# A fused attention and feed-forward layer on eight cores: feed-forward weight loads prefetched one block ahead through smaller staging buffers, and the closing layernorm taken two token tiles at a time

## The reference, cut to what matters

```python
# per sequence: x is 2048 tokens x 2048 features, float32
x = layernorm(x + attention(x))                  # 16 heads, latent q and kv, causal softmax
g   = (x @ gate_w.T) * gate_s                    # 5632 hidden features
u   = (x @ up_w.T) * up_s
hdn = silu(g) * u
x = layernorm(x + (hdn @ down_w.T) * down_s)     # eps 1e-5, no weights
```

## Time and profile before

| what | us |
|---|---|
| median of the 2 timed runs | 5615.35 (5584.98 and 5645.73) |
| the profiled execution | 5474.59 |
| its span on the slowest core (core 3) | 5472.8 |
| spans of the 8 cores | 5415.7 to 5472.8 |
| TensorE busy, share of the span | 3874.9, 71% |
| VectorE busy | 1907.8, 35% |
| ScalarE busy | 1626.9, 30% |

### The profile page before, as it was taken

One profiled execution on the slowest core, in us unless ns is written; L12 is line 12 of the kernel. 1 busy time (PEld: TensorE's weight loads), 2 busy tenths in 40 slices (PEclk: granted clock), 3 DMA queues, 4 the chain that ended last, 5 costly groups with the idle time before them and its releaser, 6 DMA issues.

```text
span 5472.8 us, 67555 instructions; the slowest of 8 cores (5415.7 to 5472.8 us)
## 1 busy us (share of the span) xinstructions
PE 3874.9 (71%) x20400; PEld 1835.9 (34%) x20400; DVE 1907.8 (35%) x4134; ACT 1626.9 (30%) x3184; POOL 318.4 (6%) x581
## 2 busy tenths in 40 slices
PE   0566577666666666666477698868879688868986
PEld 0223232233333333333133233333334233433343
DVE  2222223544444444443233333233322333233323
ACT  0011100035555555555101233223322233223322
POOL 0000000000000000000000011111111111101111
PEclk9877788878888788877688899989999899989998
DMA  4111111000000000000411588758876788758975
GB/s 124 54 39 32 55 53 47 14 14 7 7 7 9 7 7 7 8 2 25 138 39 47 177 269 252 251 177 261 254 246 215 210 254 249 244 181 253 272 236 180
DMA packets 207283, 673.46 MB, mean 123 GB/s; under 512 B 30240, under 2 KB 30752, under 8 KB 202848
## 3 DMA queue, kind: packets, MB, share of 16 engines
q1 hardware_dynamic: 120528, 340.64, 20.6%
q0 software_dynamic: 78928, 310.68, 18.0%
q10 hardware_dynamic: 7488, 17.83, 1.2%
HBM read 652.01 MB, written 16.78 MB: 122 GB/s over the span
## 4 chain that ended last, share of the span: by engine, by line
PE 36%; DMA 33%; DVE 12%; issue 10%; ACT 7%; DVEq 1%; SPq 0%; ACTq 0%; POOL 0%; POOLq 0%
DMA stg_gp<-up_l 21%; PE pD L1178 6%; PE pPT L584 5%; DMA stg_gp<-down_c 5%; PE pOP L964 5%; PE pQA L494 3%; ACT Ebuf L869 3%; PE pO L818 3%; ACT PTsb L841 3%; PE pPT L834 2%; DVE ubf L244 2%; PE pS L781 2%; PE pS L792 2%; DMA stage<-ow_l 2%; DVE stats L799 2%
## 5 line engine op out<-in xcount | busy, mean ns | idle before, releaser
L1095 PE MATMUL pG<-OX,gbf 128*128 128x512 bf16 x2816 | 676.9, 396 | 292.4 <-DVE tmid L1122 277.7
L1178 PE MATMUL pD<-h_fm,dbf 128*128 128x512 bf16 x2816 | 642.4, 385 | 114.4 <-DVE dbf L244 75.9
L1104 PE MATMUL pU<-OX,ubf 128*128 128x512 bf16 x2816 | 636.5, 379 | 0.0
L244 DVE CAST ubf<-stg_gp 128x1024 bf16<-128x1024 f32 x352 | 243.6, 693 | 963.1 <-DMA stg_gp<-up_l 922.3
L235 ACT CAST gbf<-stg_sy 128x1024 bf16<-128x1024 f32 x352 | 353.9, 1043 | 647.7 <-PE pG L1095 572.9
L1095 PEld LDWEIGHTS pG<-OX,gbf 128*128 128x128 bf16 x2816 | 276.8, 101 | 681.3 <-issue 402.1
L818 PE MATMUL pO<-PTsb,vtm 128*128 128x128 bf16 x2176 | 240.4, 240 | 313.4 <-ACT PTsb L841 307.1
L1178 PEld LDWEIGHTS pD<-h_fm,dbf 128*128 128x128 bf16 x2816 | 274.5, 99 | 460.8 <-issue 165.4
L841 ACT CAST PTsb<-pPT 128x512 bf16<-128x512 f32 (+3 forms) x640 | 313.0, 525 | 270.9 <-PE pPT L834 270.3
L1104 PEld LDWEIGHTS pU<-OX,ubf 128*128 128x128 bf16 x2816 | 275.6, 98 | 332.2
L869 ACT ACTIVATE Ebuf<-pS,stats 128x512 bf16<-128x512 f32 (+3 forms) x512 | 314.3, 621 | 207.0 <-DVE stats L860 201.9
(11 more groups left out here) (133 smaller groups left out, 3744.4 us busy)
## 6 DMA issues: line engine op xcount, KB each, us to landing
stg_gp<-up_l POOLq DMA_DIRECT2D x352, 512.0 KB, 6.4
stg_sy<-gate_l SPq DMA_DIRECT2D x352, 512.0 KB, 6.6
stg_sy<-down_c SPq DMA_DIRECT2D x128, 512.0 KB, 6.1
stg_gp<-down_c POOLq DMA_DIRECT2D x128, 512.0 KB, 5.5
stg_sy<-down_c SPq DMA_DIRECT2D x64, 384.0 KB, 7.1
stg_gp<-down_c POOLq DMA_DIRECT2D x64, 384.0 KB, 4.1
stage<-x SPq DMA_DIRECT2D x64, 256.0 KB, 3.1
xst<-x POOLq DMA_DIRECT2D x16, 1024.0 KB, 5.1
```

Source lines behind the costliest of these rows:

```text
L244: e.tensor_copy(d[:, a:a + cc], tiles[i][:, 0:cc]), inc=cP)
L1095: P.op("tensor", lambda e, wi=wi, d=d, gc0=gc0: e.matmul(pG[wi][:], gbf[wi][:, d * 128:(d + 1) * 128], OX[:, d * S + gc0:d * S + gc0 + 512 ...
L1104: P.op("tensor", lambda e, wi=wi, d=d, gc0=gc0: e.matmul(pU[wi][:], ubf[wi][:, d * 128:(d + 1) * 128], OX[:, d * S + gc0:d * S + gc0 + 512 ...
L1178: P.op("tensor", lambda e, di=di, hh=hh, jj=jj, ii=ii: e.matmul(pD[di][:], dbf[hh][:, jj * 128:(jj + 1) * 128], h_fm[:, ii * 512:(ii + 1) ...
```

## The change

Four things are done in the feed-forward half; the arithmetic is the same.

- `gu_loads` runs one block ahead: block 0 at the head of each group, block `ii + 1` behind the matmuls of `ii`. Nothing of the next group is loaded ahead of the down stage.
- The staging slots shrink: `gp` from 2x1024 to 2x768 columns, `sy2` from 3x1024 to 3x512. A block of up is then 3 chunks (768, 768, 512) where it was 2, of gate 4 where it was 2; a half of down is 4 chunks on `gp` (3 before) and 6 on `sy2` (3 before).
- `outst` is two buffers, with a semaphore each for their stores.
- The layernorm takes the 4 token tiles as two pairs, each step for both tiles of a pair before the next step.

```diff
-            outst = [sbF("outst0", [128, D], F32)] * 2
+            outst = [sbF("outst0", [128, D], F32), sbF("outst1", [128, D], F32)]
...
-            lc_gp = mk_path(sbF, "gp", "gpsimd", "vector")
-            lc_sy = mk_path(sbF, "sy2", "sync", "scalar", nslots=3)
+            lc_gp = mk_path(sbF, "gp", "gpsimd", "vector", slot_cols=768)
+            lc_sy = mk_path(sbF, "sy2", "sync", "scalar", nslots=3, slot_cols=512)
...
-            pre2 = {0: gu_loads(0), 1: gu_loads(1)}
             for grp in range(NGRP):
                 gc0 = grp * 512
...
+                pre = gu_loads(0)
...
-                    g_ready, u_ready = pre2.pop(ii)
+                    g_ready, u_ready = pre
...
-                    if ii + 2 < IC:
-                        pre2[ii + 2] = gu_loads(ii + 2)
+                    if ii + 1 < IC:
+                        pre = gu_loads(ii + 1)
...
-                if grp + 1 < NGRP:
-                    pre2[0] = gu_loads(0)
-                    pre2[1] = gu_loads(1)
...
-                for tc in range(4):
+                for pair0 in (0, 2):
+                    tcs = (pair0, pair0 + 1)
...
-                    out_free[0] = out_free[1] = (dOut, dOut.n)
+                    for tc in tcs:
+                        t_abs = grp * 4 + tc
+                        sem_o = dOut if tc % 2 == 0 else dOut2
+                        P.w("gpsimd", vE, ap[tc])
+                        P.op("gpsimd", lambda e, t_abs=t_abs, tc=tc: e.dma_start(
+                            out=out_hbm[t_abs * 128:(t_abs + 1) * 128, :],
+                            in_=outst[tc % 2][:]), inc=sem_o, k=16)
+                        out_free[tc % 2] = (sem_o, sem_o.n)
```

More of the change, by code:

```diff
@@ L148, in build_program @@
         dOut = P.sem("dOut")
+        dOut2 = P.sem("dOut2")
         dDump = P.sem("dDump")
@@ L1074, in build_program, with gu_loads @@
             HALF = IC // 2
[L1076 to L1082, removed]
-            pre2 = {0: gu_loads(0), 1: gu_loads(1)}
             for grp in range(NGRP):
                 gc0 = grp * 512
+                def gu_loads(ii):
+                    wi = ii % 2
+                    P.wf("scalar", gbf_free[wi])
+                    g_ready = lc_sy(gate_l[ii], gbf[wi], 0, D)
+                    P.wf("vector", ubf_free[wi])
+                    u_ready = lc_gp(up_l[ii], ubf[wi], 0, D)
+                    return g_ready, u_ready
+                pre = gu_loads(0)
                 P.w("tensor", vE, a4_done_v)
@@ L1201, in build_program @@
                 h_free = (tMM, d_mm)
-                for tc in range(4):
-                    t_abs = grp * 4 + tc
+                for pair0 in (0, 2):
+                    tcs = (pair0, pair0 + 1)
+                    bs = {tc: 10 + 6 * (tc % 2) for tc in tcs}
                     P.w("vector", vE, x2tm_ready)
-                    P.op("vector", lambda e, tc=tc: e.reduce_sum(
-                        stats[:, 10:11], x2tm[:, tc * D:(tc + 1) * D], axis=AX), inc=vStat)
-                    P.w("vector", vStat, vStat.n)
[L1208 to L1211, removed]
+                    for tc in tcs:
+                        b = bs[tc]
+                        P.op("vector", lambda e, tc=tc, b=b: e.reduce_sum(
+                            stats[:, b:b + 1], x2tm[:, tc * D:(tc + 1) * D],
+                            axis=AX), inc=vStat)
+                    P.w("vector", vStat, vStat.n)
+                    for tc in tcs:
+                        b = bs[tc]
+                        P.op("vector", lambda e, b=b: e.tensor_scalar_mul(
+                            stats[:, b + 1:b + 2], stats[:, b:b + 1], -1.0 / D), inc=vStat)
+                        P.op("vector", lambda e, b=b: e.tensor_scalar_mul(
+                            stats[:, b + 4:b + 5], stats[:, b:b + 1], 1.0 / D), inc=vStat)
                     nm_done = vStat.n
@@ L1214, in build_program @@
                     P.w("scalar", vStat, nm_done)
[L1215 to L1222, removed]
+                    sq_n = {}
@@ new lines, in build_program @@
+                    for tc in tcs:
+                        b = bs[tc]
+                        P.wf("scalar", out_free[tc % 2])
+                        P.op("scalar", lambda e, tc=tc, b=b: e.activation(
+                            outst[tc % 2][:], x2tm[:, tc * D:(tc + 1) * D], AF.Square,
+                            bias=stats[:, b + 1:b + 2],
+                            accum_out=stats[:, b + 2:b + 3]), inc=sAct)
+                        sq_n[tc] = sAct.n
+                    for tc in tcs:
+                        b = bs[tc]
+                        P.w("vector", sAct, sq_n[tc])
+                        P.op("vector", lambda e, b=b: e.tensor_scalar(
+                            stats[:, b + 3:b + 4], stats[:, b + 2:b + 3], 1.0 / D,
+                            EPS_LN, op0=ALU.mult, op1=ALU.add), inc=vStat)
@@ L1223, in build_program @@
                     P.w("vector", vStat, vStat.n)
-                    P.op("vector", lambda e: e.reciprocal(stats[:, 13:14], stats[:, 13:14]), inc=vStat)
+                    for tc in tcs:
+                        b = bs[tc]
+                        P.op("vector", lambda e, b=b: e.reciprocal(
+                            stats[:, b + 3:b + 4], stats[:, b + 3:b + 4]), inc=vStat)
                     P.w("scalar", vStat, vStat.n)
-                    P.op("scalar", lambda e: e.activation(
-                        stats[:, 13:14], stats[:, 13:14], AF.Sqrt), inc=sAct)
@@ L1228, in build_program @@
[L1228 to L1237, removed]
@@ L1238, in build_program @@
-                    out_free[0] = out_free[1] = (dOut, dOut.n)
+                    sq2 = {}
+                    for tc in tcs:
+                        b = bs[tc]
+                        P.op("scalar", lambda e, b=b: e.activation(
+                            stats[:, b + 3:b + 4], stats[:, b + 3:b + 4], AF.Sqrt),
+                            inc=sAct)
+                        sq2[tc] = sAct.n
+                    ap = {}
+                    for tc in tcs:
+                        b = bs[tc]
+                        P.w("vector", sAct, sq2[tc])
+                        P.op("vector", lambda e, tc=tc, b=b: e.tensor_scalar(
+                            outst[tc % 2][:], x2tm[:, tc * D:(tc + 1) * D],
+                            stats[:, b + 4:b + 5], stats[:, b + 3:b + 4],
+                            op0=ALU.subtract, op1=ALU.mult), inc=vE)
+                        ap[tc] = vE.n
@@ L1241, in build_program @@
             P.w("gpsimd", dOut, dOut.n)
+            P.w("gpsimd", dOut2, dOut2.n)
             P.w("gpsimd", dDump, dDump.n)
```

## The result

The changed kernel takes 5833.12 us (median of 11 runs, 5797.09 to 5958.22); the kernel before, timed beside it, 5568.53 us (10 runs). The ratio is 1.0608, with a 95% interval from 1.0548 to 1.0669: slower by 6%. The forecast was slower, 5776 us, +2.9%; the time lies in its range, but the move is twice as large as the sum.

A forecast was written before the change was run, and what follows sets the result against it. The trip time of up chunks, two at a time, was taken to bound the gate and up stage. 106 + 64 - 21 + 21 - 4 - 5 = +161 us gave 5636 us, scaled to 5776 us (+2.9%), range 5590 to 5930.

The forecast's parts named there:

- part 1: Gate and up stage: smaller slots lengthen the block period from 8.1 to 8.7 us, +106 us, between -35 and +246.
- The estimate from the fixed cost: Gate and up stage: from about 2 us fixed per DMA, landing 4.9 us, period 9.2 us, +194 us in place of +106.
- Gate at 7.2 us a block: Gate path: 4 chunks through 3 slots, landing after 4.2 us, take 7.2 us a block, staying under up's 8.7.
- Part 2: VectorE order, `tmid` behind fewer casts: 0 in the rate, idle time moves from gate to up; -4 us a group at stage end.
- Parts 3: Down stage: smaller slots add waits on both halves, +1.0 us a block, +64 us, between -20 and +140.
- 4: From gate and up to down: the stall goes in three groups, the first half comes later in all four, -21 us.
- 5: From down to next group: +7 us a boundary, +21 us for three; the very last layernorm -5 us.
- A: Gate and up stage: up trips under 4.15 us, 7.4 us a block, -132 us, 5483 us, faster than before; chance 0.12.
- B: A wash: gate and up periods stay at 8.1 us, the down stage pays half, +23 us, 5638 us; chance 0.24.
- C: Both ends bad: up landing 5.1 us and down waits add up in full, +377 us, 5992 us; chance 0.08.
- D: The layernorm decides through its store wait: gain 28 us at most, under 1%, unable to turn the sum; no chance given.

The follow-up runs named there:

- inplace: one_ahead with the layernorm's squares written over the hidden activations and its result in place, without output tile: 5422.45 us, ratio 0.9732 to the kernel before.
- the last two runs: inplace with larger staging: `gp` at 4x1024, 5205.1 us, ratio 0.9377; then `gp` at 3x1024 and `sy2` at 4x1024, 5147.6 us, ratio 0.936.
- Only-sy2: The kernel before with only `sy2` at 3x512 columns, `gp` still 2x1024: 5779.43 us, ratio 1.0468.
- one_ahead: The kernel before with only the prefetch order changed to one block ahead, slots and layernorm as before: 5421.44 against 5579.09 us, ratio 0.9793.

## Why the prediction was right or wrong

*The bound and the sign: right.* That time to landing on the up path sets the stage was confirmed from both sides: smaller slots alone cost 8.2%, and larger ones give 3.8% (0.936 against 0.9732 for inplace, which has the slots of before), with the arithmetic unchanged.

*The step that was mis-sized is part 1:* "A 384 KB chunk between them is 4.65, the mean of (4.65, 4.65, 4.2) is 4.5, and the period is 1.5 x 5.75 = 8.6 us." The mean is 5.2 us, just beyond the high end of 5.1, and the period 9.5 where group 0 had 8.0: +1.5 us x 176 = +264 in place of +106. That is 158 of the 169 us by which the sum fell short. And the +1.5 is a net figure: with the small slots alone a block takes 9.9 us, +1.9, and the rest of the change, the order above all, gives 0.4 of it back (below). The 4.2 and 5.1 us of the earlier trace rows came from a stretch with another queue beside SyncE's and a busy share of 0.75, below the 0.87 of the feed-forward half; that this is why they were too low was not tested. What the runs show is that the landing time rises with the bytes that the path's own slots hold, and hardly with the size of a chunk. With 0.75 MB up chunks land after 4.9 to 5.7 us (384 KB) and 4.8 to 5.7 (256 KB), with 1 MB after 6.1 to 7.0, with 1.5 MB after 8.9, with 2 MB after 7.2 to 11.2 depending on the core. It is no exact law: 1 MB took 6.4 us beside gate slots of 1.5 MB and 7.0 beside gate slots of 0.75 MB (only `sy2` small), and in the last two runs up chunks no longer bound the stage. But from 1 MB down the landing time falls by less than the bytes do, so a path with fewer bytes in its slots is slower, however they are cut.

*The estimate from the fixed cost was nearer.* The Trainium skill, DMA: Bandwidth & Descriptors, Anatomy of one DMA, gives a fixed cost of about 2 us. The landing time and the period estimated with it were 4.9 and 9.2 us, and 5.2 and 9.5 are measured; no run here measures the fixed part by itself. The rule of the Trainium skill in the same page's section Bandwidth, to batch to 1 MiB, speaks of the single transfer; here 4x512 columns did as well as 2x1024 in the gate and up stage (352 against 351 us), so what had to be large is the sum outstanding.

*Gate at 7.2 us a block: too low, but it is not what bounds the changed kernel.* Its landing time was taken as 4.2 and is 5.1 us; by the same formula that is 4/3 x (5.1 + 1.2) = 8.4 us. Only-sy2, where gate chunks land after 5.8 us, shows it as a bound of its own, 9.0 us a block. In the changed kernel ScalarE waits for gate chunks too, but TensorE, in group 3's stage, waits for gate once, at its start, and inside the stage only for up:

```profile
PE pU L1105 <- DVE ubf L245: 95.2, 33, 10.2
...
PE pG L1096 <- ACT gbf L236: 31.5, 1, 31.5
```

*Part 2, the order at 0 in the rate: wrong.* Moving only the casts behind sigmoid, `tmid` and `h_fm` brings group 0's blocks from 8.0 to 7.4 us. My argument was that the idle time only moves from gate to up. One thing it leaves out: before, TensorE's wait ahead of gate also delays the end of that block's up matmuls, which the next casts and so the next loads wait for. But of that the waits show only some 6 us in group 0's stage, of the 24 gained there; the rest is chunks that land sooner, and its cause is not shown. So the change contains a gain of about 2% (one_ahead, 0.9793), which I had put between -10 and +20 us.

*Parts 3, 4, 5:* +80, -22 and -8 us against +64, -21 and -5. Down blocks are 13.3 us, with waits on both halves as foreseen. The boundaries can't be read apart from the rate: +280 us less 264 leaves +16, against +17 in the sum.

*The rivals.* A (trips under 4.15 us) and B did not happen. C had nearly the right landing time, 5.1 us, but not its down stage. D was right to be put aside: without the paired layernorm the ratio is 1.0626.

*The scale, and luck:* to the sum for the profiled execution, 5636 us, 141 us were added, because the two timed runs lay that far above it. The changed kernel's profiled execution took 5804.82 us, 169 more than the sum, and its median lies only 28 us above that. So the addition was too large by 112 us and hid two thirds of the miss. That 5833 us lies in the range owes more to this than to the working; without the addition the range would have ended at 5789 us.

## What to carry to other kernels

When weights are staged through slots, count the bytes that the late path keeps outstanding before counting its chunks: here time to landing rose with the bytes on the path and hardly with the size of a chunk, and SBUF taken from staging for an output tile cost 8% to win less than 1%. Before giving a tile its own buffer, see whether its data can lie over something that is dead by then; the freed space, put into staging, was worth more than every reordering. And try emitting the instructions that free a PSUM bank ahead of casts that wait for weights, even if the same chunk seems to be the bound either way; here it took 351 us down to 327.

## What the runs showed of the hardware that I had not expected

After most waits of some microseconds for an up chunk, the next 16 up matmuls take longer. In the changed kernel's profile 16 matmuls take 3.6 us when they follow the matmuls before them at once or after less than 1.5 us (79 of 79); after waits of 2 to 3 us they take 4.5 on average (32 cases, 3.6 to 5.3), after 3 to 5 us 5.3 (41 cases, 3.6 to 6.4). One such case in the timeline, and the granted clock of the same stretch and of the next (the columns of the earlier trace rows):

```profile
4129.46 5.30 PE L1105 MATMUL pU<-OX,ubf 128*128 128x512 bf16 x16 [3.54 <-DVE ubf L245]
4134.60 3.62 PE L1096 MATMUL pG<-OX,gbf 128*128 128x512 bf16 x16
...
4129.40:4134.70 5.30, 5.24 (x17) 2.13 (x18) 1.69 (x3) 2.23 (x4) 1.09 (x2) 0.68 0.57 134
4134.70:4138.10 3.40, 3.40 (x18) 1.51 (x16) 1.54 (x3) 0.62 (x1) 0.55 (x1) 1.00 0.73 252
```

The clock stood at its full level, 2.4 GHz, in the second row and for a part of the first at the lower one, 1.2 GHz (0.68 on average).

The granted clock of that stage is 0.91 of full speed where it was 0.97, and the up matmuls are busy 757.0 us in all, against 645.6 for as many gate matmuls. So waits bring slower matmuls with them, already in the kernel before, where the waits stood ahead of gate (676.9 us for gate, 636.5 for up). The prediction set the clock aside ("plays no part"); in group 0's stage TensorE is busy 337.00 us for the matmuls that took 316.33, 0.5 us a block more. How much of it lies on the path was not tried: the next chunk is late anyway.

Two slots of 1024 columns and four of 512 gave the same landing time, 6.4 us on the slowest core, in the same queue. I had expected the smaller chunk to land sooner by at least its own transfer.
